# One kernel of attention and experts: the order of VectorE's and ScalarE's work within a unit, and of the experts' turns

## The chip, the cores and the metric

The kernel runs on one core of one Trainium2 chip. The metric is the device time of one execution in microseconds (us). The kernel before took 897.06 us, the median of three runs (889.57, 897.35 and 897.06).

## The reference

A layer norm feeds two branches, whose outputs are added to the input. Shapes are 4 sequences of 1024 tokens of 128 channels; 16 heads of 8 channels; 8 experts with hidden size 256, two chosen for each token.

```
xn = layernorm(x)
# attention
s = q @ k.T ; s = s - mean(s) ; s = s / mean(|s|) * gain          # over all 1024 keys
r = max(where(causal, s, -1000), 0) ** 4
y = (r / sum(r)) @ v ; attention = y @ W_proj + b_proj
# experts, two of eight by token
z = (xn @ w1 + b1) * (xn @ w2 + b2)
s = silu(z @ wg + bg) ; expert = s @ w3 + b3
out = x + attention + sum of weight * expert
```

## The kernel before

**Units.** The main loop runs over `ALL` = 192 units: 16 quads of four heads, 12 units each. A unit n is one pair of a block of 128 keys and a half of 512 queries, for four heads. `STEPS` lists them; the blocks on the diagonal are narrower, so that positions 0 to 11 in a quad have 512, 384, 256, 128, then five times 512, then 384, 256, 128 columns. For each head of a unit TensorE makes scores (line L921), ScalarE writes `U` = relu(score) (L788), VectorE writes `W` = relu(score) times `U` (L1177), GpSimd masks the diagonal and squares one part of `W` (L660, L669), ScalarE squares the rest (L799), and two units later TensorE multiplies `W` and `U` with `VS` and a column of ones into the accumulator (`average`, L859).

**Pieces.** The mean of |s| wants the sum of the positive scores over all keys. What the units don't cover is made as "pieces" of 512 scores (L914), which are only summed, by VectorE ("V", L1169, into `junk_V`) or by ScalarE ("A", L780, into `junk_A`). `PLAN` says how many pieces lie in a unit and who takes each; up to unit 35 all are VectorE's.

**Expert turns.** 39 tiles of 256 tokens (20 pairs, the last of one tile) pass through the experts in 119 turns, spread evenly over units 35 to 179, at most one in a unit. Turns of a pair p are `tx` (transpose of the tokens, L890), `m` for each tile (two products, m1 and m2, L874), `ga` and `gb` (the gate products, L894) and `my` (the last product, L899). ScalarE evacuates tx, m1, ga and gb. VectorE evacuates m2 into `zT` (L1127) and my into `yb` (L1135). GpSimd weights `yb` (L628) and scatters its rows (L635) in the units that follow. `NWB` buffers hold the experts' weights, loaded by SyncE.

**Order.** Each engine's queue is written out by the same loop. TensorE, in unit n: pieces, four scores, the turn's product, `average` of unit n-2. ScalarE: its pieces, `U`, evacuation of the turn of unit n, squares of unit n-1. VectorE: its pieces, `W`, evacuation of the turn of unit n.

**Banks.** All products but the accumulator share a ring of `NBANK` = 7 PSUM banks, in the order of `takers`: pieces, scores and turn of a unit, then of the next. An m turn takes two banks, every other turn one. Before TensorE writes a bank it waits for the reader of what stood there seven takers ago:

```
def wait_bank(engine, *who):
    if PLACE[who] >= NBANK:
        engine.wait_ge(*last_read(takers[PLACE[who] - NBANK]))
```

With three pieces a unit has seven takers, so the fourth score of a unit stands seven takers behind the last bank of the turn of the unit ahead; with four pieces, the third score does.

Of the kernel before, what the change touches and what calls it, by code (L numbers as in the profile page):

```python
# [18 lines left out]
HALF = 512  # L19
# [15 lines left out]
def layer_kernel(nc, x, w_attn, b_attn, w_proj, b_proj, score_gain, gate_w, gate_b, w_expert, out):  # L35
# [48 lines left out]

    PLAN = ["VA", "VAV", "VAV", "VAVA", "V", "V", "V", "V", "VA", "VAV", "VAV", "VAVA"]
    EARLY = 3
# [14 lines left out]

    NXT, NWB, NYB = 6, 3, 4
    NPAIR = -(-NX // 2)
    tiles_of = lambda p: range(2 * p, min(2 * p + 2, NX))
    TURNS = []
    for p in range(NPAIR):
        TURNS += [("tx", p)] + [("m", i) for i in tiles_of(p)] + [("ga", p), ("gb", p), ("my", p)]
    FFN_FROM, FFN_TO = SCATTERS // PER_STEP + 3, ALL - 12
# [27 lines left out]
    with ctx:  # L136
# [80 lines left out]
        gat = sb("gat", [P, 2, NT, C])  # L217
        pad = NWB * WW + 2 * (2 * R + 2 * R + 4 * R + 4 * R) - 2 * NT * C
        sb("rest_of_ffn", [P, pad])
# [177 lines left out]
        def _(sp):  # L397
# [68 lines left out]
            chosen = []  # L466
            W_AT = [STEP_OF["m", i] - 8 if i < NWB else STEP_OF["my", (i - NWB) // 2] + 1 for i in range(NX)]
            T_AT = [max(SCATTERS // PER_STEP + 1, STEP_OF["tx", i // 2] - 4) for i in range(NX)]
# [76 lines left out]
        def _(pool):  # L545
# [99 lines left out]
            for n in range(ALL):  # L645
                if 0 < n * PER_STEP < SCATTERS:
                    pool.wait_ge(w_done, 4 * n - 2)
                for k in range(n * PER_STEP, min(SCATTERS, (n + 1) * PER_STEP)):
                    scatter(k // NT, k % NT)
                for back in range(1, 5):  # L650
                    for kind, p in FFN_AT[n - back] if n >= back else []:
                        if kind == "my":
                            if back == 1:
                                rows_of_pair(p)
                            if back <= 2 * len(tiles_of(p)):
                                give_back(p, back - 1)
                slot, w = W[n % NU], HALF - LOW[n % NS]
# [24 lines left out]
        def _(act):  # L682
# [79 lines left out]
            for n in range(ALL + AVLAG + 2):  # L762
                y = n - AVLAG - 1
                if y >= 0 and y % NS in ENDS:
# [7 lines left out]
                    act.copy(yq[q % 2][:, STEPS[y % NS][0], :], acc).then_inc(acc_ev, 1)  # L772
                if n < ALL:
                    for m, e in PIECE_AT[n]:
                        if e == "A":
                            act.wait_ge(p_ready, m + 1)
                            k_th, at = PIECE_COUNT[m]["A"], 0
                            wait(act, p_used["A"], k_th - 1)
                            for g, _, _, w, col in PIECES[m % NP]:
                                last = act.activation(junk["A"][k_th % 2][:, at:at + w], piece(m)[:, at:at + w], ACT.Relu,  # L780
                                                      accum_out=msum[:, m // NP, g, col:col + 1])
                                at += w
                            last.then_inc(p_used["A"], 1)
                    w = HALF - LOW[n % NS]
                    wait(act, used, n - NU + 1)
                    for g in range(4):
                        act.wait_ge(s_ready, 4 * n + g + 1)
                        act.activation(U[n % NU][:, g, 0:w], score(4 * n + g)[:, 0:w], ACT.Relu).then_inc(u_ready, 1)  # L788
                    for kind, i in FFN_AT[n]:
# [179 lines left out]
        def _(vec):  # L969
# [192 lines left out]
            for n in range(ALL):  # L1162
                for m, e in PIECE_AT[n]:
                    if e == "V":
# [3 lines left out]
                        for g, _, _, w, col in PIECES[m % NP]:  # L1168
                            last = vec.tensor_scalar(junk["V"][k_th % 2][:, at:at + w], piece(m)[:, at:at + w], 0.0, None,  # L1169
                                                     ALU.max, ALU.add, accum_out=msum[:, m // NP, g, col:col + 1])  # L1170
                            at += w
                        last.then_inc(p_used["V"], 1)
                w = HALF - LOW[n % NS]
                wait(vec, used, n - NU + 1)
                for g in range(4):
                    vec.wait_ge(u_ready, 4 * n + g + 1)
                    vec.scalar_tensor_tensor(W[n % NU][:, g, 0:w], score(4 * n + g)[:, 0:w], 0.0,  # L1177
                                             U[n % NU][:, g, 0:w], ALU.max, ALU.mult).then_inc(w_done, 1)
                for kind, i in FFN_AT[n]:
                    evacuate(kind, i)  # L1180
                for b in side(n, S_SCALE):
# [64 lines left out]
```

## Time and profile before

| what | value |
|---|---|
| median of three runs | 897.06 us (889.57 to 897.35) |
| profiled execution | 888.43 us, its span 886.7 us |
| mean granted clock of TensorE in it | 0.942 of full speed |
| TensorE busy | 740.6 us, 84% of the span |
| VectorE busy | 724.4 us, 82% |
| ScalarE busy | 683.5 us, 77% |
| GpSimd busy | 623.9 us, 70% |
| largest group, VectorE's W (L1177) | 373.8 us in 768 instructions |

The profiled execution belongs to one run; its own time is 8.6 us below the median of the three. Engine names in rows: PE is TensorE, PEld its weight loads, DVE VectorE, ACT ScalarE, POOL GpSimd, SP SyncE. A row's idle time is what its engine waited just before it, and the name behind the arrow is what ended the wait.

### The profile page before, as it was taken

The numbers are of one execution on the slowest core, as the hardware profiler recorded it, in microseconds if no ns is written. First come the engines' busy times: TensorE is split into PE (matmuls) and PEld (weight loads), VectorE is DVE, ScalarE is ACT, GpSimd is POOL, SyncE is SP. The second block draws the span as 40 slices with busy tenths as digits, with TensorE's granted clock in tenths as the row PEclk, the third lists the DMA queues.
The fourth block names the chain that finished last, engine by engine and source line by source line (L and its number), as shares of the span: only waits on it lengthen the run. The fifth ranks groups of instructions, "written<-read, shape, count | busy, mean of one in ns | idle before, by whom it ended". The sixth has DMA issues, their size and how long they took to land.

```text
span 886.7 us, 17644 instructions
## 1 busy us (share of the span) xinstructions
PE 740.6 (84%) x5719; PEld 335.2 (38%) x5719; DVE 724.4 (82%) x2043; ACT 683.5 (77%) x1639; POOL 623.9 (70%) x545
## 2 busy tenths in 40 slices
PE   0572888888999999899898989989999999989872
PEld 0530222222444454444344344444434444443222
DVE  7689898989777978786876977787787977778896
ACT  0573888888987878898886787888888887878870
POOL 5262777884897687686876776787777777778773
PEclk9995797979998999999999899999999999999895
DMA  8449703155325304250523423252323605230703
GB/s 270 136 190 264 307 32 85 43 156 156 59 83 167 114 18 131 84 129 19 141 85 59 146 72 70 90 141 85 58 91 99 179 11 141 82 57 10 215 6 101
DMA packets 60330, 97.10 MB, mean 110 GB/s; under 512 B 7360, under 2 KB 39744, under 8 KB 60240
## 3 DMA queue, kind: packets, MB, share of 16 engines
q1 hardware_dynamic: 54544, 86.22, 34.1%
q0 software_dynamic: 4544, 9.38, 3.3%
q8 instruction: 45, 0.74, 0.4%
q10 hardware_dynamic: 1152, 0.40, 0.2%
q14 instruction: 45, 0.37, 0.1%
HBM read 61.29 MB, written 34.36 MB: 108 GB/s over the span
## 4 chain that ended last, share of the span: by engine, by line
PE 45%; DVE 23%; ACT 13%; issue 12%; POOL 4%; DMA 1%; DVEq 1%; SPq 0%; ACTq 0%; POOLq 0%
PE bank L859 19%; DVE W L1177 10%; PE bank L894 7%; ACT U L788 7%; PE bank L874 6%; DVE junk_V L1169 5%; PE bank L914 4%; PE bank L899 3%; ACT W L799 3%; PE bank L921 2%; ACT junk_A L780 2%; POOL W L660 1%; POOL W L669 1%; DVE zT L1127 1%; POOL sorted_x L610 1%
## 5 line engine op out<-in xcount | busy, mean ns | idle before, releaser
L1177 DVE SCALAR_TENSOR_TENSOR W<-bank,U 128x512 f32<-128x512 f32 (+3 forms) x768 | 373.8, 549 | 40.1 <-ACT U L788 38.0
L788 ACT ACTIVATE U<-bank 128x512 f32<-128x512 f32 (+3 forms) x768 | 318.5, 519 | 48.3 <-PE bank L921 35.3
L859 PE MATMUL bank<-W,VS 128*10 128x512 f32 (+3 forms) x1536 | 297.8, 507 | 13.5 <-ACT yq L772 7.2
L859 PE MATMUL bank<-U,usel 128*10 128x512 f32 (+3 forms) x1536 | 292.7, 507 | 0.0
L1169 DVE TENSOR_SCALAR_CACHE_REDUCE junk_V<-bank 128x512 bf16<-128x512 f32 (+3 forms) x445 | 218.3, 533 | 88.2 <-PE bank L914 87.5
L669 POOL TENSOR_TENSOR W<-W 128x1024 f32<-128x1024 f32 (+2 forms) x159 | 231.6, 1460 | 53.9 <-DVE W L1177 45.9
L660 POOL TENSOR_TENSOR W<-W,causal 128x512 f32<-128x512 f32 x128 | 163.6, 1278 | 108.5 <-DVE W L1177 106.9
L799 ACT ACTIVATE W<-W 128x256 f32<-128x256 f32 (+2 forms) x225 | 191.6, 880 | 10.4 <-POOL W L660 10.2
L921 PE MATMUL bank<-QS,KS 48*128 48x512 bf16 (+3 forms) x768 | 162.9, 337 | 39.3 <-DVE W L1177 17.3
L780 ACT ACTIVATE junk_A<-bank 128x512 bf16<-128x512 f32 (+3 forms) x195 | 87.7, 460 | 57.2 <-PE bank L914 56.8
L914 PE MATMUL bank<-KS,QS 48*128 48x512 bf16 (+3 forms) x640 | 102.0, 328 | 17.0 <-DVE junk_V L1169 8.5
L921 PEld LDWEIGHTS bank<-QS,KS 48*128 48x128 bf16 x768 | 56.4, 95 | 110.8 <-DVE W L1177 60.8
L859 PEld LDWEIGHTS bank<-U,usel 128*10 128x10 f32 x1536 | 59.5, 92 | 86.2 <-issue 79.4
L635 POOL DMA_INDIRECT weighted_y<-yb,row_to x78 | 79.3, 1016 | 14.7 <-issue 9.0
L874 PE MATMUL bank<-xT,wb 128*128 128x256 f32 x312 | 82.1, 409 | 7.0 <-DVE junk_V L1169 4.6
L914 PEld LDWEIGHTS bank<-KS,QS 48*128 48x128 bf16 x640 | 29.2, 95 | 153.8 <-issue 109.5
L894 PE MATMUL bank<-zT,wb 128*128 128x256 f32 x312 | 78.8, 396 | 7.6 <-DVE junk_V L1169 5.5
L859 PEld LDWEIGHTS bank<-W,VS 128*10 128x10 f32 x1536 | 59.9, 92 | 66.3 <-issue 36.9
L610 POOL DMA_INDIRECT sorted_x<-xn_row,pos x64 | 62.8, 981 | 18.0 <-issue 14.5
L874 PEld LDWEIGHTS bank<-xT,wb 128*128 128x128 f32 x312 | 58.9, 199 | 24.6 <-issue 16.9
L894 PEld LDWEIGHTS bank<-zT,wb 128*128 128x128 f32 x312 | 57.0, 193 | 24.9 <-issue 13.9
L758 ACT ACTIVATE sT<-bank,wb 128x256 f32<-128x256 f32 x78 | 33.3, 483 | 20.4 <-PE bank L894 20.3
(158 smaller groups left out, 604.5 us busy)
## 6 DMA issues: line engine op xcount, KB each, us to landing
wb<-in_experts SPq DMA_DIRECT2D x39, 707.0 KB
qk_stacked<-parts SPq DMA_DIRECT2D x8, 768.0 KB, 11.7
QS<-qk_stacked SPq DMA_DIRECT2D x32, 192.0 KB
KS<-qk_stacked SPq DMA_DIRECT2D x32, 192.0 KB
xt_all<-sorted_x SPq DMA_DIRECT2D x39, 130.0 KB, 6.0
qk_stacked<-parts SPq DMA_DIRECT2D x8, 512.0 KB, 11.7
gat<-weighted_y SPq DMA_DIRECT2D x8, 512.0 KB, 6.6
sorted_x<-xt_all SPq DMA_DIRECT2D x3, 1300.0 KB, 11.7
```

Of the source, the lines that this page charges most:

```text
L660: pool.tensor_tensor(slot[:, :, 0:P], slot[:, :, 0:P], causal[:, :].unsqueeze(1).to_broadcast([P, 4, P]), ALU.mult).then_inc(w_mask, 1)
L669: pool.tensor_tensor(some, some, some, ALU.mult).then_inc(r_ready[n % NU], 1)
L780: last = act.activation(junk["A"][k_th % 2][:, at:at + w], piece(m)[:, at:at + w], ACT.Relu, accum_out=msum[:, m // NP, g, col:col + 1])
L788: act.activation(U[n % NU][:, g, 0:w], score(4 * n + g)[:, 0:w], ACT.Relu).then_inc(u_ready, 1)
L799: act.activation(some, some, ACT.Square).then_inc(r_ready[y % NU], 1)
L859: last = pe.matmul(acc[32 * g:32 * g + VW, lo:HALF], usel[:, :] if of_u else VS[q % 2][:, j, g, :], (U if of_u else W)[n % NU][:, g, 0:HAL ...
L874: last = pe.matmul(bank_of(part, k)[:, h * R:(h + 1) * R], w[:, at + h * P:at + (h + 1) * P], moving, start=True, stop=True)
L894: last = pe.matmul(to[:, at:at + R], w[:, in_w:in_w + P], zT[k % 2][:, i % 2, h, :], start=(h == 0), stop=(h == 1))
L914: last = pe.matmul(piece(m)[:, at:at + w], QS[par][in_rows[g % 2], g // 2, P * t:P * (t + 1)], KS[par][in_rows[g % 2], g // 2, k:k + w], s ...
L921: pe.matmul(score(4 * n + g)[:, 0:HALF - lo], KS[par][in_rows[g % 2], g // 2, P * j:P * (j + 1)], QS[par][in_rows[g % 2], g // 2, HALF * c ...
L1169: last = vec.tensor_scalar(junk["V"][k_th % 2][:, at:at + w], piece(m)[:, at:at + w], 0.0, None, ALU.max, ALU.add, accum_out=msum[:, m // ...
L1177: vec.scalar_tensor_tensor(W[n % NU][:, g, 0:w], score(4 * n + g)[:, 0:w], 0.0, U[n % NU][:, g, 0:w], ALU.max, ALU.mult).then_inc(w_done, 1)
```

## The change

VectorE's queue in unit n becomes: its pieces, evacuation of the turn of unit n-1, `W`. ScalarE's becomes: `U`, its pieces, evacuation of the turn of unit n, squares. The pieces' table puts V ahead of A within a unit, with the same number of each. The turns of two pairs are interleaved, so that `my` of pair p-1 lies between the two m turns of pair p, and `tx` of pair p+1 between the second m and `ga`. GpSimd's weighting and scatters of a pair begin one unit later, a fourth weight buffer is added, and a weight load is issued one unit later after the `my` that frees its buffer.

```diff
-    PLAN = ["VA", "VAV", "VAV", "VAVA", "V", "V", "V", "V", "VA", "VAV", "VAV", "VAVA"]
+    PLAN = ["VA", "VVA", "VVA", "VVAA", "V", "V", "V", "V", "VA", "VVA", "VVA", "VVAA"]
...
-    NXT, NWB, NYB = 6, 3, 4
+    NXT, NWB, NYB = 6, 4, 4
...
-    TURNS = []
+    TURNS = [("tx", 0)]
     for p in range(NPAIR):
-        TURNS += [("tx", p)] + [("m", i) for i in tiles_of(p)] + [("ga", p), ("gb", p), ("my", p)]
+        first, *second = [("m", i) for i in tiles_of(p)]
+        TURNS += [first] + [("my", p - 1)] * (p > 0) + second + [("tx", p + 1)] * (p + 1 < NPAIR) + [("ga", p), ("gb", p)]
+    TURNS.append(("my", NPAIR - 1))
...
-            W_AT = [STEP_OF["m", i] - 8 if i < NWB else STEP_OF["my", (i - NWB) // 2] + 1 for i in range(NX)]
+            W_AT = [STEP_OF["m", i] - 8 if i < NWB else STEP_OF["my", (i - NWB) // 2] + 2 for i in range(NX)]
...
-                for back in range(1, 5):
+                for back in range(2, 6):
...
                 if n < ALL:
+                    w = HALF - LOW[n % NS]
+                    wait(act, used, n - NU + 1)
+                    for g in range(4):
+                        act.wait_ge(s_ready, 4 * n + g + 1)
+                        act.activation(U[n % NU][:, g, 0:w], score(4 * n + g)[:, 0:w], ACT.Relu).then_inc(u_ready, 1)
                     for m, e in PIECE_AT[n]:
...
-                    w = HALF - LOW[n % NS]
-                    wait(act, used, n - NU + 1)
-                    for g in range(4):
-                        act.wait_ge(s_ready, 4 * n + g + 1)
-                        act.activation(U[n % NU][:, g, 0:w], score(4 * n + g)[:, 0:w], ACT.Relu).then_inc(u_ready, 1)
...
                         last.then_inc(p_used["V"], 1)
+                for kind, i in FFN_AT[n - 1] if n else []:
+                    evacuate(kind, i)
                 w = HALF - LOW[n % NS]
...
-                for kind, i in FFN_AT[n]:
-                    evacuate(kind, i)
```

VectorE's queue around units 36 to 38, before. The first two rows evacuate m2 of unit 36; then come the two pieces and `W` of unit 37, m2 of unit 37, and the first piece of unit 38.

```order
L1127 SCALAR_TENSOR_TENSOR zT0<-bank2,wb0,x1_0 128x256 [waits ffn_m1_evacuated,ffn_m2_done]
L1127 SCALAR_TENSOR_TENSOR zT0<-bank2,wb0,x1_0 128x256
L1169 TENSOR_SCALAR junk_V1,msum<-bank3 128x512 [waits piece_used_vec,piece_ready]
L1169 TENSOR_SCALAR junk_V0,msum<-bank0 128x512 [waits piece_used_vec,piece_ready]
L1177 SCALAR_TENSOR_TENSOR W1<-bank1,U1 128x384 [waits u_ready,u_and_r_used]
L1177 SCALAR_TENSOR_TENSOR W1<-bank1,U1 128x384 [waits u_ready]
L1177 SCALAR_TENSOR_TENSOR W1<-bank2,U1 128x384 [waits u_ready] x2
L1127 SCALAR_TENSOR_TENSOR zT0<-bank0,wb1,x1_1 128x256 [waits ffn_m1_evacuated,ffn_m2_done]
L1127 SCALAR_TENSOR_TENSOR zT0<-bank0,wb1,x1_1 128x256
L1169 TENSOR_SCALAR junk_V1,msum<-bank0 128x512 [waits piece_used_vec,piece_ready]
```

The same place after the change. The pieces of a unit now stand ahead of the evacuation of the unit before it, and that one ahead of `W`.

```order
L1171 TENSOR_SCALAR junk_V1,msum<-bank3 128x512 [waits piece_used_vec,piece_ready]
L1171 TENSOR_SCALAR junk_V0,msum<-bank0 128x512 [waits piece_used_vec,piece_ready]
L1129 SCALAR_TENSOR_TENSOR zT0<-bank2,wb0,x1_0 128x256 [waits ffn_m1_evacuated,ffn_m2_done]
L1129 SCALAR_TENSOR_TENSOR zT0<-bank2,wb0,x1_0 128x256
L1181 SCALAR_TENSOR_TENSOR W1<-bank1,U1 128x384 [waits u_ready,u_and_r_used]
L1181 SCALAR_TENSOR_TENSOR W1<-bank1,U1 128x384 [waits u_ready]
L1181 SCALAR_TENSOR_TENSOR W1<-bank2,U1 128x384 [waits u_ready] x2
L1171 TENSOR_SCALAR junk_V1,msum<-bank0 128x512 [waits piece_used_vec,piece_ready]
L1171 TENSOR_SCALAR junk_V0,msum<-bank1 128x512 [waits piece_used_vec,piece_ready]
L1129 SCALAR_TENSOR_TENSOR zT0<-bank0,wb1,x1_1 128x256 [waits ffn_m1_evacuated,ffn_m2_done]
```

TensorE's queue of unit 38 up to its turn, before: three pieces, four scores, and the start of ga.

```order
L914 MATMUL bank0<-KS1,QS1 128x512 [waits piece_used_vec]
L914 MATMUL bank1<-KS1,QS1 128x512 [waits w_done] x2
L921 MATMUL bank2<-QS1,KS1 128x256 [waits w_done] x2
L921 MATMUL bank3<-QS1,KS1 128x256 [waits ffn_m1_evacuated]
L921 MATMUL bank0<-QS1,KS1 128x256 [waits ffn_m2_evacuated]
L894 MATMUL bank0<-zT0,wb0 128x256 [waits piece_used_vec,ffn_m2_evacuated]
```

The same place in the changed kernel.

```order
L916 MATMUL bank0<-KS1,QS1 128x512 [waits piece_used_act]
L916 MATMUL bank1<-KS1,QS1 128x512 [waits w_done] x2
L923 MATMUL bank2<-QS1,KS1 128x256 [waits w_done] x2
L923 MATMUL bank3<-QS1,KS1 128x256 [waits ffn_m1_evacuated]
L923 MATMUL bank0<-QS1,KS1 128x256 [waits ffn_m2_evacuated]
L892 MATMUL bank0<-ident,xt_all 128x128 [waits ffn_x_in2,piece_used_vec]
```

Pieces and scores stay where they were, and so does the wait of the fourth score (the last row but one) for the evacuation of m2 of unit 37; the turn behind it is tx where it was ga.

ScalarE's queue of unit 37 before: piece, `U`, and the squares behind them.

```order
L780 ACTIVATE junk_A0,msum<-bank0 128x512 [waits piece_used_act,piece_ready]
L788 ACTIVATE U1<-bank1 128x384 [waits scores_ready,u_and_r_used]
L788 ACTIVATE U1<-bank1 128x384 [waits scores_ready]
L788 ACTIVATE U1<-bank2 128x384 [waits scores_ready] x2
L799 ACTIVATE W0<-W0 128x1024 [waits w_masked] x2
```

ScalarE's queue from the evacuation of m1 of unit 36 through unit 37 in the changed kernel.

```order
L752 ACTIVATE x1_0<-bank2,wb2 128x256 [waits ffn_m2_evacuated,ffn_m1_done]
L752 ACTIVATE x1_0<-bank2,wb2 128x256
L780 ACTIVATE U1<-bank1 128x384 [waits scores_ready,u_and_r_used]
L780 ACTIVATE U1<-bank2 128x384 [waits scores_ready] x2
L780 ACTIVATE U1<-bank3 128x384 [waits scores_ready]
L787 ACTIVATE junk_A0,msum<-bank1 128x512 [waits piece_used_act,piece_ready]
L801 ACTIVATE W0<-W0 128x1024 [waits w_masked] x2
```

The piece has moved from ahead of `U` to behind it.

## Rows read from the trace of the kernel before

**Rows 1.** The page, part 1: busy time, share, instructions of each engine.
```profile
PE 740.6 (84%) x5719; PEld 335.2 (38%) x5719; DVE 724.4 (82%) x2043; ACT 683.5 (77%) x1639; POOL 623.9 (70%) x545
```

**Rows 2.** The page, part 4: the chain that ended last.
```profile
PE 45%; DVE 23%; ACT 13%; issue 12%; POOL 4%; DMA 1%; DVEq 1%; SPq 0%; ACTq 0%; POOLq 0%
```

**Rows 3.** Windows: the stretch with expert turns; busy us of each engine, then clock.
```profile
core 0: us, PE busy (x) PEld busy (x) DVE busy (x) ACT busy (x) POOL busy (x), PEclk, DMA share, GB/s
...
280.00:760.00 480.00, 442.28 (x3530) 214.45 (x3522) 383.23 (x1048) 393.77 (x1010) 355.78 (x310) 0.98 0.34 94
```

**Rows 4.** Waits, 280 to 790 us: total us, times, longest.
```profile
DVE junk_V L1169 <- PE bank L914: 65.3, 59, 2.4
...
DVE W L1177 <- ACT U L788: 29.4, 62, 1.3
```

**Rows 5.** Timeline, unit 37: start, us, engine, instruction, idle time before it.
```profile
219.69 0.60 PE L914 MATMUL bank<-KS,QS 48*128 48x512 bf16 x3
...
220.16 0.86 DVE L1127 SCALAR_TENSOR_TENSOR zT<-bank,wb,x 128x256 f32<-128x256 f32 x2
...
220.95 0.68 DVE L1169 TENSOR_SCALAR_CACHE_REDUCE junk_V<-bank 128x512 bf16<-128x512 f32 x1
...
221.08 0.33 PE L921 MATMUL bank<-QS,KS 48*128 48x384 bf16 x1 [0.45 <-DVE zT L1127]
...
221.78 1.97 PE L874 MATMUL bank<-xT,wb 128*128 128x256 f32 x8 [0.36 <-DVE junk_V L1169]
```

**Rows 6.** Timeline, units 81 and 82.
```profile
402.74 0.86 DVE L1127 SCALAR_TENSOR_TENSOR zT<-bank,wb,x 128x256 f32<-128x256 f32 x2
...
403.23 0.60 PE L914 MATMUL bank<-KS,QS 48*128 48x512 bf16 x3
...
403.46 0.70 PE L921 MATMUL bank<-QS,KS 48*128 48x384 bf16 x4
403.65 0.69 DVE L1169 TENSOR_SCALAR_CACHE_REDUCE junk_V<-bank 128x512 bf16<-128x512 f32 x1
...
404.50 1.97 PE L874 MATMUL bank<-xT,wb 128*128 128x256 f32 x8 [0.34 <-DVE junk_V L1169]
...
404.88 1.95 DVE L1177 SCALAR_TENSOR_TENSOR W<-bank,U 128x384 f32<-128x384 f32 x4
...
408.23 0.55 PE L914 MATMUL bank<-KS,QS 48*128 48x512 bf16 x4
...
409.50 1.97 PE L894 MATMUL bank<-zT,wb 128*128 128x256 f32 x8 [0.45 <-DVE junk_V L1169]
...
409.96 1.41 DVE L1177 SCALAR_TENSOR_TENSOR W<-bank,U 128x256 f32<-128x256 f32 x4
```

**Rows 7.** Timeline, unit 83, of four pieces.
```profile
413.24 0.61 PE L914 MATMUL bank<-KS,QS 48*128 48x256 bf16 x8
...
413.66 0.42 DVE L1169 TENSOR_SCALAR_CACHE_REDUCE junk_V<-bank 128x256 bf16<-128x256 f32 x1 [2.29 <-PE bank L914]
...
414.50 0.23 PE L921 MATMUL bank<-QS,KS 48*128 48x128 bf16 x1 [0.54 <-DVE junk_V L1169]
...
414.69 1.97 PE L894 MATMUL bank<-zT,wb 128*128 128x256 f32 x8
```

**Rows 8.** Timeline, unit 60, a unit of one piece on each engine.
```profile
319.13 0.39 PE L914 MATMUL bank<-KS,QS 48*128 48x512 bf16 x2
...
319.89 1.99 PE L894 MATMUL bank<-zT,wb 128*128 128x256 f32 x8
...
320.88 2.48 DVE L1177 SCALAR_TENSOR_TENSOR W<-bank,U 128x512 f32<-128x512 f32 x4 [0.62 <-ACT U L788]
```

**Rows 9.** The line of yb: instructions, ns min/median/max, first and last start.
```profile
L1135 DVE TENSOR_TENSOR yb<-bank,wb x39: 410/411/426, 241.0 to 815.6; 128x256 f32<-128x256 f32 x39
```

**Rows 10.** Windows before and in a fall of the clock, columns as in rows 3.
```profile
148.00:151.00 3.00, 1.32 (x7) 0.43 (x11) 3.00 (x7) 3.00 (x5) 2.01 (x4) 1.00 0.07 22
151.00:154.50 3.50, 3.50 (x20) 0.59 (x13) 2.60 (x6) 3.50 (x7) 2.59 (x4) 0.57 0.17 51
```

More of the change, by code:

```diff
@@ L217, in layer_kernel @@
         gat = sb("gat", [P, 2, NT, C])
-        pad = NWB * WW + 2 * (2 * R + 2 * R + 4 * R + 4 * R) - 2 * NT * C
+        pad = NWB * (WW + 10) + 2 * (2 * R + 2 * R + 4 * R + 4 * R) - 2 * NT * C
         sb("rest_of_ffn", [P, pad])
@@ L649, in _ @@
                     scatter(k // NT, k % NT)
-                for back in range(1, 5):
+                for back in range(2, 6):
                     for kind, p in FFN_AT[n - back] if n >= back else []:
                         if kind == "my":
-                            if back == 1:
+                            if back == 2:
                                 rows_of_pair(p)
-                            if back <= 2 * len(tiles_of(p)):
-                                give_back(p, back - 1)
+                            if back - 2 < 2 * len(tiles_of(p)):
+                                give_back(p, back - 2)
                 slot, w = W[n % NU], HALF - LOW[n % NS]
```

## The prediction

> **What bounds the kernel now.** I read the page first: TensorE is busy 84% of the span, VectorE 82%, ScalarE 77% [rows 1], and the chain that ended last lies on TensorE for 45% and on VectorE for 23% [rows 2]. An average hides stages, so next the windows. Up to unit 35 nothing that the change touches happens (all pieces are VectorE's, there is no turn, and `U` has no piece to pass), and units behind 180 have no turn. In the stretch with turns TensorE is busy 442.3 of 480 us at a granted clock of 0.98 [rows 3]. So it idles 37.7 us there; that is nearly all that a better order could win, and every new wait of TensorE is added to the time, unless another engine is late at the same place.
>
> VectorE is what TensorE's order leans on. It waits 65.3 us for pieces, 59 times, and 29.4 us for `U`, 62 times [rows 4]. The first of these waits matters: behind `W`, VectorE has nothing to do until TensorE has finished turn and average, and in that gap it now evacuates the turn. Unit 80's m2 is evacuated from 402.74 to 403.60 while TensorE averages and begins the pieces of unit 81 at 403.23 [rows 6]. That evacuation costs nothing.
>
> **VectorE: the evacuation behind the next unit's pieces.** Seven banks make a ring. In a unit of three or four pieces the fourth or third score uses the bank of the turn of the unit ahead. The order of the changed kernel shows it for unit 38: its last score waits for m2 of unit 37, and VectorE now comes to that only behind its two pieces of unit 38. The same wait stands in the kernel before, where it is mostly long over. Where it isn't, the trace has its signature: in unit 37 VectorE ends m2 of unit 36 at 221.02 and the score starts at 221.08, 0.45 us late [rows 5]. So a freed bank is used 0.06 us later.
>
> The price, by unit 82 [rows 6]. TensorE starts its pieces at 408.23, VectorE has summed its pieces at 409.96 (there `W` starts). Now m2 of unit 81 follows, 0.86 us as at 402.74: 410.82. The score starts 0.06 us later, and the turn 0.19 us behind it (414.50 to 414.69, [rows 7]): 411.07, where it started at 409.50. That is 1.57 us; taken as 1.55. For `my` the evacuation is two instructions of 0.41 us [rows 9]: in unit 81 VectorE's pieces end at 404.88, so 404.88 + 0.82 + 0.06 + 0.19 = 405.95 against 404.50 [rows 6], 1.45 us. A unit of four pieces has the same columns for VectorE, and its turn starts 1.45 us behind its first piece [rows 7], not earlier than the 1.27 us in unit 82; I take the same price. VectorE can't catch up behind it: `W` of unit 82 would end 0.9 us later, but TensorE's next pieces come 1.5 us later.
>
> How often: from the two tables of turns and takers, a score of the next unit stands on the bank of an m2 in 19 units and on that of a `my` in 10. The count was 29 before too; what changes is VectorE's place in each. Five of these lie in position 1 of a quad, where VectorE is late already. In unit 37 the turn started 2.09 us behind the first piece [rows 5]. With the new order VectorE goes to the pieces at 220.16, needs 1.23 us for them (403.65 to 404.88, [rows 6]), then 0.86 + 0.06 + 0.19: 222.50 against 221.78, 0.7 us. The sum: 15 x 1.55 + 9 x 1.45 + 5 x 0.7 = 39.8, say **+39**. A stall that falls into one that exists would cost nothing, and the full price is the other end: 0 to 45.
>
> **Smaller terms of the same kind.** In positions 0 and 8 (two pieces) it is the next turn that stands on the bank. In unit 60 the turn starts at 319.89, 0.76 us behind the first piece at 319.13 [rows 8]; VectorE would free the bank about 0.43 + 0.62 + 0.86 + 0.06 = 1.97 us behind it. That is 1.2 us in seven units, and 7 with some of it hidden behind VectorE in position 0. In units of four pieces the turn waits for VectorE's second piece where it waited for ScalarE's first, some 0.4 us in the 12 of them that have no stall yet: 5. ScalarE's pieces are now read behind `U`, so that their banks come free some 2 us later; only with a short turn or none is TensorE there by then: 2. Together **+14** (3 to 20).
>
> **ScalarE: U ahead of its pieces.** In unit 60 `W` waits 0.62 us for `U`, which stands behind a piece [rows 8]. That wait goes, but in most units VectorE then waits for TensorE anyway. I count 0.4 us in 13 units of position 0, **-5**, with 0 and the whole 29.4 us [rows 4] as ends. The pieces' table (V ahead of A) leaves counts alone and lets VectorE begin both its pieces sooner; without it the stall would be longer, and it has no price of its own.
>
> **Interleaved turns, GpSimd, SyncE.** The number of turns, their products and their spacing stay. `ga` gets tx between it and the m2 that it needs; this covers the later evacuation, and without it `ga` would wait as the scores do. `my` lies at least one turn further from `gb`. GpSimd's weighting and its scatters come one unit later; behind them in its queue are the mask and the square of the same unit, as before, and their cover is two units until the average. The fourth buffer lets each weight load be issued some four units ahead of its m turn; its wait stands in SyncE's queue ahead of loads of tokens and of a quad's stores and loads. TensorE waited for no weight load in this trace. I cost these at nothing; if the cover were gone, one late load in each of 20 pairs would cost about a microsecond each (0 to 20).
>
> **The clock.** At 148 to 151 us TensorE was busy 1.32 of 3.00 us, and in the 3.5 us that follow the granted clock was 0.57, mostly its lower level of 1.2 GHz [rows 10]. A fall costs (1 - 0.57) x 3.5 = 1.5 us of its work. The stretch with turns has few falls now (0.98, [rows 3]), and its idle time comes in bits of half a microsecond. The new stalls are 1.6 us idle in one piece at 24 places. I take five falls, **+8**; 0 to 30 are the ends.
>
> The Trainium skill (TensorE: Matmul & The Clock Gate, A second HAM failure mode: psum-queue depth-cycling) says that a kernel which cycles through PSUM banks can leave TensorE idle so often for short times that its clock goes up and down. By that rule the falls would be many and not five, which is the second rival below; the rows of the stretch with turns don't show it so far.
>
> **The sum.** 39 + 14 - 5 + 8 = +56. On the profiled execution (888.4) this gives 944. The three runs lie at 889.6, 897.1 and 897.4; their median is 8.6 us above the profiled one. Since either level may come, I add to the middle of the runs, 893.5: **950 us**. Its own range is 930 to 970.
>
> **The rivals.**
> 1. *Half absorbed.* TensorE's existing idle 37.7 us are partly at the same scores, and VectorE, which enters each unit free, may do its pieces sooner than in these rows. With half of 39 and 14, no falls and -5: 893.5 + 21 = 915. For it: unit 37, where half the price was there already. Against: only five of 29 places lie in that position.
> 2. *The clock falls at most stalls.* 15 more falls of 1.5 us: 950 + 22 = 972. For it: rows 10. Against: one fall needs not follow each stall; the windows at 148 had idle time of more than one wait.
> 3. *Faster.* ScalarE's `U` first is the edit that counts: VectorE waits 29.4 us for it, and if VectorE is the engine that ends the units, about half of that goes straight to the end, with evacuations hidden while `U` is made: 893.5 - 16 = 877. The point from which it decides: the last score of a unit would have to come 2.5 us behind its first piece anyway, so that the evacuation is over. In unit 82 the turn, behind all scores, starts at 1.27 us [rows 6], so the rows speak against it.
> 4. *No change.* Stalls and savings cancel, the order of TensorE being bound by the sum of its products: 893.
>
> **Chances.** Forecast 0.52, half absorbed 0.20, clock 0.12, faster 0.08, no change 0.08. Slower by over 1% (which is about what a measurement of this kernel can tell from no change) holds the first three: 0.84. The range reaches from 905 (below the first rival) to 985 (above the second, for the ends of the clock's term) and leaves out the last two.
>
> **What would show it.** In the profile after: TensorE's scores waiting for zT and yb, 29 times and about 1.6 us each, some 40 us where there were few; VectorE's wait for pieces longer; its wait for `U` shorter; TensorE's share of the stretch with turns near 0.86 and more slices of its clock below 9. Wrong would be: waits for zT of half a microsecond, or a fourth score that starts no later than before; then VectorE reaches the evacuation sooner than I think, or another engine sets the pace.

## The result and the profile after

The changed kernel takes 980.43 us, the median of four runs (975.05 to 980.80), against 894.60 us for four runs of the kernel before (889.57 to 897.35). The ratio is 1.0952, with an interval of 1.0884 to 1.1021. The profiled execution took 980.13 us, with a span of 978.4 us and a mean clock of 0.91 (before: 888.43, 886.7 and 0.942).

First the page: engines (part 1) and the chain that ended last (part 4), which answer to [rows 1, 2].

```profile
PE 776.8 (79%) x5719; PEld 347.7 (36%) x5719; DVE 721.6 (74%) x2043; ACT 689.3 (70%) x1639; POOL 623.8 (64%) x545
...
PE 54%; DVE 25%; issue 12%; ACT 7%; DMA 1%; DVEq 1%; SPq 0%; ACTq 0%
```

TensorE's busy time rose from 740.6 to 776.8 us with the same 5719 matmuls, so 36.2 us are the same work at a lower clock. The rest of the span, in which TensorE is idle, rose from 146.1 to 201.6 us, by 55.5. The two make the 91.7 us of the span. VectorE and ScalarE do the same work in nearly the same time; their shares fell. The window of the stretch with turns (columns as in [rows 3], where it showed 442.28 busy and a clock of 0.98; being slower, the kernel gets through fewer units in it):

```profile
280.00:760.00 480.00, 409.64 (x3061) 195.64 (x3060) 331.14 (x916) 347.70 (x891) 307.68 (x267) 0.93 0.29 81
```

The same work is compared by taking each kernel from its first score of unit 35 to its first score of unit 180, here before and then after:

```profile
212.11:819.71 607.60, 557.27 (x4453) 268.86 (x4451) 483.55 (x1342) 499.95 (x1286) 454.98 (x391) 0.98 0.32 89
```

```profile
216.04:911.60 695.56, 593.73 (x4453) 280.72 (x4451) 481.64 (x1343) 505.04 (x1286) 453.61 (x388) 0.93 0.27 77
```

So the whole 36 us of busy time lie in this part. In the record of the granted clock it has 4 stretches at the lower level before and 25 after.

What TensorE waited for is in the view of waits (engine, line, releaser: total us, times, longest).

```profile
DVE junk_V L1171 <- PE bank L916: 204.7, 118, 4.6
...
PE bank L923 <- DVE zT L1129: 35.5, 19, 2.1
...
PE bank L923 <- DVE yb L1137: 17.4, 10, 1.9
...
DVE W L1181 <- ACT U L780: 14.0, 41, 1.3
...
PE bank L923 <- DVE junk_V L1171: 12.5, 27, 0.5
...
PE bank L896 <- DVE junk_V L1171: 8.0, 18, 0.6
...
PE bank L916 <- ACT junk_A L787: 5.3, 7, 1.3
```

The evacuations of zT and yb now hold up scores in 19 and 10 places, for 35.5 and 17.4 us: 1.87 and 1.74 us each. Before, the same two releasers stood ahead of scores for 1.3 and 0.6 us. VectorE's wait for pieces, 87.5 us before over the whole span, is 204.7: it is free early and stands idle until TensorE gets on. Its wait for `U` fell from 38.0 to 14.0 us and bought nothing.

Unit 37 in the timeline (start us, us, engine, instruction, idle time before it) answers to [rows 5].

```profile
225.22 0.60 PE L916 MATMUL bank<-KS,QS 48*128 48x512 bf16 x3
...
225.64 0.69 DVE L1171 TENSOR_SCALAR_CACHE_REDUCE junk_V<-bank 128x512 bf16<-128x512 f32 x1 [0.41 <-PE bank L916]
...
226.87 0.87 DVE L1129 SCALAR_TENSOR_TENSOR zT<-bank,wb,x 128x256 f32<-128x256 f32 x2
227.66 1.94 DVE L1181 SCALAR_TENSOR_TENSOR W<-bank,U 128x384 f32<-128x384 f32 x4
...
227.80 0.33 PE L923 MATMUL bank<-QS,KS 48*128 48x384 bf16 x1 [1.65 <-DVE zT L1129]
...
228.06 2.83 PE L876 MATMUL bank<-xT,wb 128*128 128x256 f32 x8
```

TensorE begins its pieces at 225.22, VectorE has summed both at 226.87, evacuates m2 of unit 36 until 227.74, and 0.06 us later the fourth score starts, 1.65 us late. The turn starts 2.84 us behind the first piece; before it was 2.09. The turn itself then takes 2.83 us where it took 1.97. That is the clock, and unit 38 shows it again behind the next stall: these are its fourth score and a row of two matmuls of the average that follows, 0.60 us at the upper level.

```profile
234.60 0.28 PE L923 MATMUL bank<-QS,KS 48*128 48x256 bf16 x1 [1.77 <-DVE zT L1129]
...
236.64 1.07 PE L861 MATMUL bank<-W,VS 128*10 128x512 f32 x2
```

The windows of these units (columns as in [rows 3]) put the clock beside it.

```profile
225.00:229.00 4.00, 2.35 (x19) 1.31 (x12) 3.59 (x10) 2.82 (x8) 3.16 (x2) 1.00 0.00 0
229.00:232.00 3.00, 3.00 (x23) 1.55 (x24) 0.59 (x2) 2.08 (x6) 2.25 (x2) 0.51 0.00 0
232.00:235.00 3.00, 1.23 (x9) 0.44 (x6) 2.56 (x8) 1.54 (x5) 0.50 (x1) 0.92 0.11 20
235.00:238.50 3.50, 3.50 (x21) 0.65 (x21) 0.86 (x3) 2.10 (x5) 2.48 (x3) 0.63 0.80 169
```

TensorE is busy 2.35 of 4.00 us around the first stall, and then 3 us are granted at 0.51, the lower level of 1.2 GHz; it is busy 1.23 of 3.00 us around the second, and 0.63 follows. Of the 29 stalls, 1.53 to 2.07 us long, 19 have a stretch at the lower level that begins within 2 us of the score that ends them; the other ten have none. [rows 10] showed the same pattern in the kernel before, in a part without turns.

### The profile page after: what moved, and what is told of

It is laid out like the page before. It is cut to its first block, busy times and chain, and to the rows that moved or that the text cites. A ratio compares the mean times of both kernels' runs of the same rounds, so it can differ in the third digit from the quotient of the medians.

```text
span 978.4 us, 17644 instructions
## 1 busy us (share of the span) xinstructions
PE 776.8 (79%) x5719; PEld 347.7 (36%) x5719; DVE 721.6 (74%) x2043; ACT 689.3 (70%) x1639; POOL 623.8 (64%) x545
## 4 chain that ended last, share of the span: by engine, by line
PE 54%; DVE 25%; issue 12%; ACT 7%; DMA 1%; DVEq 1%; SPq 0%; ACTq 0%
PE bank L861 22%; PE bank L876 8%; DVE W L1181 8%; PE bank L896 8%; DVE junk_V L1171 7%; PE bank L916 5%; PE bank L901 4%; PE bank L923 3%; ACT U L780 3%; DVE zT L1129 3%; ACT W L801 2%; DVE yb L1137 1%; ACT junk_A L787 1%; PE bank L832 1%; DMA x_t<-in_L_attn_x 1%
## 5 line engine op out<-in xcount | busy, mean ns | idle before, releaser
L780 ACT ACTIVATE U<-bank 128x512 f32<-128x512 f32 (+3 forms) x768 | 323.5, 510 | 192.6 <-PE bank L923 176.3
L1171 DVE TENSOR_SCALAR_CACHE_REDUCE junk_V<-bank 128x512 bf16<-128x512 f32 (+3 forms) x445 | 218.7, 534 | 204.9 <-PE bank L916 204.7
L861 PE MATMUL bank<-W,VS 128*10 128x512 f32 (+3 forms) x1536 | 313.8, 529 | 14.2 <-ACT W L801 7.1
L861 PE MATMUL bank<-U,usel 128*10 128x512 f32 (+3 forms) x1536 | 308.7, 530 | 0.0
L923 PE MATMUL bank<-QS,KS 48*128 48x512 bf16 (+3 forms) x768 | 163.0, 337 | 78.9 <-DVE zT L1129 35.5
L916 PE MATMUL bank<-KS,QS 48*128 48x512 bf16 (+3 forms) x640 | 106.0, 334 | 24.0 <-DVE junk_V L1171 9.1
L876 PE MATMUL bank<-xT,wb 128*128 128x256 f32 x312 | 88.0, 427 | 8.3 <-DVE junk_V L1171 4.4
L896 PE MATMUL bank<-zT,wb 128*128 128x256 f32 x312 | 81.1, 404 | 11.0 <-DVE junk_V L1171 8.0
L901 PE MATMUL bank<-wb,sT 128*128 128x128 f32 x312 | 47.0, 313 | 3.7 <-DVE zT L1129 2.5
## 6 DMA issues: line engine op xcount, KB each, us to landing
sorted_x<-xt_all SPq DMA_DIRECT2D x3, 1300.0 KB, 11.5
```

The source lines that it names most:

```text
L861: last = pe.matmul(acc[32 * g:32 * g + VW, lo:HALF], usel[:, :] if of_u else VS[q % 2][:, j, g, :], (U if of_u else W)[n % NU][:, g, 0:HAL ...
L876: last = pe.matmul(bank_of(part, k)[:, h * R:(h + 1) * R], w[:, at + h * P:at + (h + 1) * P], moving, start=True, stop=True)
L896: last = pe.matmul(to[:, at:at + R], w[:, in_w:in_w + P], zT[k % 2][:, i % 2, h, :], start=(h == 0), stop=(h == 1))
L916: last = pe.matmul(piece(m)[:, at:at + w], QS[par][in_rows[g % 2], g // 2, P * t:P * (t + 1)], KS[par][in_rows[g % 2], g // 2, k:k + w], s ...
L923: pe.matmul(score(4 * n + g)[:, 0:HALF - lo], KS[par][in_rows[g % 2], g // 2, P * j:P * (j + 1)], QS[par][in_rows[g % 2], g // 2, HALF * c ...
```

## The experiments

Theory: VectorE's evacuation behind the next unit's pieces makes the loss, through the bank that a score of that unit wants, partly as idle time and partly through the clock that falls behind it. Rival A: ScalarE's `U` first costs too, since its pieces' banks come free late. Rival B: the interleaved turns cost. Rivals C and D: the clock's falls follow the idle time and count, or they don't. The kernels ran on three chips, each beside the kernel before: the changed kernel with the evacuation in its own unit and the three "before" kernels down to the pieces' table beside one of 892.91 us, the turns alone, the evacuation behind the first piece, the average first and the three zero matmuls beside one of 907.45, the rest beside one of 905.74. So ratios are compared and not times, and the forecasts, made in us beside about 895, are read as ratios too.

| kernel | ratio to before | interval |
|---|---|---|
| changed | 1.0952 | 1.0884 to 1.1021 |
| changed, evacuation in its own unit | 1.0141 | 1.0101 to 1.0180 |
| before, evacuation moved alone | 1.0867 | 1.0820 to 1.0913 |
| before, U first alone | 1.0503 | 1.0438 to 1.0569 |
| before, U first and the pieces' table | 1.0091 | 1.0055 to 1.0127 |
| before, turns, buffer, GpSimd's rows alone | 0.9982 | 0.9943 to 1.0020 |
| changed, evacuation behind the first piece | 1.0536 | 1.0503 to 1.0568 |
| changed, average ahead of the blocked score | 1.0402 | 1.0367 to 1.0437 |
| changed, three zero matmuls in the stall | 1.0879 | 1.0846 to 1.0912 |
| changed, two | 1.0668 | 1.0619 to 1.0717 |
| changed, one | 1.0633 | 1.0585 to 1.0681 |
| changed, again, beside those two | 1.0845 | 1.0792 to 1.0898 |
| changed, evacuation by unit | 1.0207 | 1.0159 to 1.0254 |

**The evacuation back in its own unit.**

```diff
-                for kind, i in FFN_AT[n - 1] if n else []:
-                    evacuate(kind, i)
                 w = HALF - LOW[n % NS]
...
+                for kind, i in FFN_AT[n]:
+                    evacuate(kind, i)
                 for b in side(n, S_SCALE):
```

> The changed kernel with VectorE's evacuation of the turn put back behind W of its own unit; U first, the pieces' table, the turns, the fourth buffer stay. Theory (the evacuation behind the next unit's pieces makes the whole loss, by the ring of banks): TensorE's 29 waits for zT and yb go from 52.9 us to under 4, its busy time from 777 back to about 740 since the clock falls less, and the time is 885 to 902. Rival A (U ahead of ScalarE's pieces frees their banks late and costs too): 905 to 925. Rival B (the interleaved turns cost): the same 905 to 925, told apart by the kernels with one part each.

Measured: 904.98 us, ratio 1.0141. Scores wait for zT 2.6 us in all, 6 times, and for yb not at all; TensorE's busy time is back (page, part 1):

```profile
PE 735.9 (82%) x5719; PEld 333.3 (37%) x5719; DVE 724.6 (81%) x2043; ACT 685.4 (76%) x1639; POOL 623.4 (69%) x545
```

So this one placement carries eight of the nine and a half per cent, with all of the clock's part. 1.4% stay: 904.98 lies above the 885 to 902 of the theory and at the edge of rival A's 905 to 925, and as a ratio (1.012 to 1.034) inside it. Rival A holds for this rest, as the kernel with `U` first and the table shows below.

**The evacuation moved alone,** with the opposite diff on the kernel before.

> The kernel before with one edit: VectorE evacuates the turn of unit n-1 between pieces and W of unit n. The old turns also have 29 scores on a bank of m2 or my. Theory: 29 waits of 1.6 to 1.9 us each and as many falls of the clock, and ga behind the second m now waits for zT in units where it follows at once: 965 to 990. Rival (the loss needs the interleaved turns or U first with it): below 940.

Measured: 969.93 us, ratio 1.0867. The waits (columns as above):

```profile
PE bank L921 <- DVE zT L1127: 35.5, 19, 2.1
...
PE bank L921 <- DVE yb L1135: 17.2, 10, 2.0
...
PE bank L894 <- DVE zT L1127: 10.5, 9, 1.2
```

The time lies in the 965 to 990 that I expected. These are the same 19 and 10 places and the same sizes as in the changed kernel, with the old turns. So it needs neither the interleaved turns nor `U` first. The third row is what the interleaving is for: without tx between the second m and ga, nine ga turns wait 10.5 us for zT.

**U first alone.**

```diff
                 if n < ALL:
+                    w = HALF - LOW[n % NS]
+                    wait(act, used, n - NU + 1)
+                    for g in range(4):
+                        act.wait_ge(s_ready, 4 * n + g + 1)
+                        act.activation(U[n % NU][:, g, 0:w], score(4 * n + g)[:, 0:w], ACT.Relu).then_inc(u_ready, 1)
                     for m, e in PIECE_AT[n]:
                         if e == "A":
...
```

> The kernel before with one edit: ScalarE makes U ahead of its pieces. My prediction put -5 us on it (889); VectorE's wait for U falls from 38 us to about 14. Rival A: ScalarE's pieces are summed up to 2 us later, TensorE waits for their banks, and the time is 900 to 915.

Measured: 936.07 us, ratio 1.0503. I had expected a gain of 5 us; this is the largest miss of the study. It is beyond rival A too, which gave 900 to 915. Who waited for ScalarE's pieces (L785 in this kernel), from the view of that line:

```profile
  PE bank L874: 16.0, 18
...
  PE bank L894: 9.6, 8
  PE bank L914: 9.1, 12
  PE bank L899: 3.6, 3
```

TensorE waits 38.3 us for them in these four rows; before it was 1.0. In "VAV" and "VAVA" the second piece is ScalarE's, and its bank is wanted next by the second product of an m turn or by a ga, gb, my or tx in the same unit. While the piece stood ahead of `U`, it was read in time. Behind four activations of `U` it isn't.

**U first with the pieces' table.**

```diff
-    PLAN = ["VA", "VAV", "VAV", "VAVA", "V", "V", "V", "V", "VA", "VAV", "VAV", "VAVA"]
+    PLAN = ["VA", "VVA", "VVA", "VVAA", "V", "V", "V", "V", "VA", "VVA", "VVA", "VVAA"]
...
```

> The kernel before with U ahead of ScalarE's pieces and the pieces' table V ahead of A. Theory: within 1% of before (886 to 903). Rival A: as with U alone or worse, since in a unit of four pieces the turn waits for VectorE's second piece: 900 to 915.

Measured: 900.60 us, ratio 1.0091, within the 1% that I expected. The table gives back four of the five per cent: VectorE's second piece now stands on the bank that is wanted first. What is left of the waits:

```profile
PE bank L894 <- DVE junk_V L1169: 9.9, 22, 0.6
...
PE bank L874 <- DVE junk_V L1169: 8.8, 20, 0.6
...
PE bank L914 <- ACT junk_A L785: 7.8, 10, 1.3
```

ga, gb (L894) and m (L874) wait 18.7 us for VectorE's pieces, where these two waited 10.1 before, and pieces (L914) wait 7.8 us for ScalarE's. Together, `U` first and its table cost 0.9% and save no time. TensorE's idle time, span less busy time, is 161.8 us here and 161.7 in the changed kernel with the evacuation in its own unit, where it was 146.1 before: the rest that stayed there is mainly this pair.

**The turns alone.** The kernel before with `NXT, NWB, NYB`, `TURNS`, `W_AT` and `range(2, 6)` of the change.

> The kernel before with the interleaved turns, the fourth weight buffer, the later weight loads and GpSimd's rows one unit later; VectorE's and ScalarE's queues and the pieces' table as before. Theory: ga no longer waits for zT (1.3 us before), nothing else: 885 to 900. Rival B: the turns bring waits of their own: 905 or more.

Measured: 905.00 us beside 907.45, ratio 0.9982: no difference. The time alone would touch rival B's 905, but the kernel before is slower on this chip. Rival B falls. The parts add up: 8.7% for the evacuation, 0.9% for `U` and table, nothing for the turns, against 9.5% for all.

**Behind the first piece.** The evacuation stands ahead of VectorE's second piece.

```diff
...
                         last.then_inc(p_used["V"], 1)
-                for kind, i in FFN_AT[n - 1] if n else []:
-                    evacuate(kind, i)
+                        if not evacuated:
+                            evacuated = True
+                            for kind, i in FFN_AT[n - 1] if n else []:
+                                evacuate(kind, i)
```

> The changed kernel with the evacuation moved ahead of VectorE's second piece, behind its first. In units of three or four pieces the bank comes free 0.6 to 0.7 us sooner. Theory (the time is the wait for the bank): the 29 waits fall from 1.8 to 1.2 us each, 18 us less, and the clock falls somewhat less often: 945 to 965. Rival C (the clock falls at any such stall and its falls are most of the loss): 965 to 978. If the stall isn't on the path: 980.

Measured: 952.67 us, ratio 1.0536. The theory gave 945 to 965 beside about 895, ratios of 1.056 to 1.079, so this is a little better than forecast. Its waits, and then the page's row of TensorE:

```profile
PE bank L923 <- DVE zT L1129: 23.3, 19, 1.4
...
PE bank L923 <- DVE yb L1137: 10.9, 10, 1.3
```

```profile
PE 757.8 (80%) x5719; PEld 336.5 (35%) x5719; DVE 721.8 (76%) x2043; ACT 689.8 (73%) x1639; POOL 623.1 (66%) x545
```

The 29 waits fell by 18.7 us to 34.2, as expected. TensorE's busy time is 757.8 us, where two profiles of the changed kernel have 776.8 and 773.2, and the turns alone, on the same chip as this one, 746.4. A stall shorter by a third lost half of the clock's part or more: the two shrink together, not one for the other. The stretches at the lower level between units 35 and 180 are 9, where those two profiles have 25 and 18.

**Zero matmuls in the stall.** They read `U` against a stationary of zeros and add nothing to the accumulator, so the result is the same.

```diff
                     for g in range(4):
+                        of = takers[PLACE["score", 4 * n + g] - NBANK] if PLACE["score", 4 * n + g] >= NBANK else ("", 0)
+                        if of[0] in ("m2", "my") and of in [(k if k != "m" else "m2", i) for k, i in FFN_AT[n - 1]] and n % NS in (1, 3, 9, 10, 11):
+                            for _ in range(3):
+                                pe.matmul(acc[0:9, 0:HALF], usel[:, 0:9], U[(n - 3) % NU][:, 0, :], start=False, stop=False,
+                                          skip_group_check=True)
                         wait_bank(pe, "score", 4 * n + g)
```

> The changed kernel with three matmuls of 512 columns against a stationary of zeros, added to the accumulator (they add nothing), ahead of the score that waits for the bank, in 23 of the 29 places (position 2 of a quad is left out). They take about 1.3 us and lie in the stall. Rival C (falls of the clock follow the idle time and cost TensorE 36 us of busy time): the clock stays at its upper level, the time falls by 20 to 35 us, to 945 to 960, although work is added. Rival D (the clock falls for another reason, or its falls are hidden in other waits): 978 to 990.

Measured: 984.39 us, ratio 1.0879. The time lies in rival D's 978 to 990, the ratio between the two forecasts, and it can't be told from the changed kernel's. The timeline shows why: three of them (six instructions) run 2.74 us and not the 1.3 that I had reckoned with, and the score that waited for a bank before starts right behind them without a wait.

```profile
410.40 2.74 PE L925 MATMUL bank<-U,usel 128*9 128x512 f32 x6
413.08 0.33 PE L928 MATMUL bank<-QS,KS 48*128 48x384 bf16 x1
413.34 1.99 PE L876 MATMUL bank<-xT,wb 128*128 128x256 f32 x8
```

They add some 0.9 us to each of 23 stalls, about 20 us. The page's row of TensorE has the gain that this hides:

```profile
PE 818.8 (83%) x5857; PEld 348.1 (35%) x5857; DVE 723.2 (74%) x2043; ACT 688.9 (70%) x1639; POOL 623.0 (63%) x545
```

Without 23 x 2.74 us the kernel's own matmuls take 755.8, some 20 us less than in the changed kernel. Then two and one of them were run, with the changed kernel beside them.

> The changed kernel with two of the zero matmuls, not three, ahead of the blocked score in 23 of the 29 places. Three took 2.74 us in the trace, 0.9 us more than the wait that they fill; two take 1.83 us, about the wait. Rival C (the clock's falls follow the idle time): added work is hidden and the falls are mostly gone, 20 to 30 us below the changed kernel run beside it. Rival D (the clock doesn't matter): no more than 3 us from it.

> The same with one zero matmul, 0.91 us of a wait of 1.8 us. It can add nothing to the path. Rival C: the idle time in one piece is halved, and 10 to 30 us of the clock's falls go; rival D: no change from the changed kernel.

> The changed kernel itself, on the chip of the two kernels with zero matmuls, to compare them on one chip: its ratio to the kernel before again 1.09 to 1.10.

Measured: two 966.36 us (1.0668), one 964.57 us (1.0633), the changed kernel 982.75 us (1.0845). Work was added, and 16 us went with two (20 to 30 were expected, at most 3 by rival D), 18 us with one (10 to 30 expected). TensorE's row on the page of the changed kernel on this chip, then with one, then with two:

```profile
PE 773.2 (79%) x5719; PEld 343.7 (35%) x5719; DVE 722.6 (74%) x2043; ACT 689.9 (70%) x1639; POOL 623.9 (64%) x545
```

```profile
PE 774.9 (81%) x5765; PEld 335.0 (35%) x5765; DVE 722.5 (75%) x2043; ACT 688.3 (72%) x1639; POOL 623.0 (65%) x545
```

```profile
PE 792.7 (82%) x5811; PEld 340.8 (35%) x5811; DVE 722.7 (75%) x2043; ACT 688.9 (71%) x1639; POOL 623.9 (65%) x545
```

One zero matmul (two instructions) is 1.03 us of busy time in the timeline below, so 23 of them are 23.7 us of the 774.9; the kernel's own matmuls took 751.2, against 773.2 without: 22 us less. The idle time fell from 206.8 to 185.2 us, which is about the zero matmuls' own time. So the score starts as late as it did, and what went is the slower clock behind it. Between units 35 and 180 (windows as above, the changed kernel on this chip, then with one):

```profile
227.45:913.08 685.63, 581.76 (x4451) 275.42 (x4448) 481.78 (x1343) 504.89 (x1286) 453.62 (x388) 0.95 0.27 78
```

```profile
225.03:891.03 666.00, 582.41 (x4497) 267.92 (x4493) 481.66 (x1343) 503.71 (x1286) 453.13 (x388) 0.98 0.28 80
```

Less 23.7, the own matmuls take 558.7 us there, against 557.27 in the kernel before: all of the clock's part is gone. The stretches at the lower level fell from 18 to 5. In unit 37 of the kernel with one, the turn that had taken 2.83 us takes 1.99:

```profile
233.47 1.03 PE L925 MATMUL bank<-U,usel 128*9 128x512 f32 x2
235.19 0.33 PE L928 MATMUL bank<-QS,KS 48*128 48x384 bf16 x1 [0.70 <-DVE zT L1134]
235.46 1.99 PE L876 MATMUL bank<-xT,wb 128*128 128x256 f32 x8
```

That decides for rival C: the clock's falls follow TensorE's idle time in the stalls, and they cost on the path. Whether it is the length of one piece of idle time that counts or its sum around the place is not shown; a zero matmul shortens both. Two of them take 1.89 us:

```profile
237.31 1.89 PE L925 MATMUL bank<-U,usel 128*9 128x512 f32 x4
239.13 0.33 PE L928 MATMUL bank<-QS,KS 48*128 48x384 bf16 x1
```

Then the kernel's own matmuls take 792.7 - 23 x 1.89 = 749.2 us, about the same as with one.

**The average ahead of the blocked score.** TensorE does the average of unit n-2 in the stall and not behind the turn.

```diff
                     for g in range(4):
+                        of = takers[PLACE["score", 4 * n + g] - NBANK] if PLACE["score", 4 * n + g] >= NBANK else ("", 0)
+                        if not averaged and of in [(k if k != "m" else "m2", i) for k, i in (FFN_AT[n - 1] if n else []) if k in ("m", "my")]:
+                            averaged = True
+                            averages(n - AVLAG)
                         wait_bank(pe, "score", 4 * n + g)
...
```

> The changed kernel in which TensorE, in the 29 units whose third or fourth score stands on the bank of the turn ahead, does the average of unit n-2 ahead of that score and not behind the turn. The average (0.6 to 1.8 us) fills the stall. Theory: most of the wait and of the clock's falls go: 905 to 935, the rest being later U and W of those units. If the bank isn't the reason: 980.

Measured: 942.61 us beside 907.45, ratio 1.0402. I had expected 905 to 935 beside about 895, ratios up to 1.045. What is left of the scores' waits for zT and yb, 35.5 and 17.4 us before:

```profile
PE bank L937 <- DVE zT L1137: 8.4, 10, 1.1
...
PE bank L937 <- DVE yb L1145: 3.0, 6, 1.0
```

```profile
PE 765.0 (81%) x5719; PEld 340.9 (36%) x5719; DVE 721.1 (77%) x2043; ACT 686.7 (73%) x1639; POOL 623.2 (66%) x545
```

Real work in the stall takes away more than half of the loss, which confirms the bank. Beside the turns alone (902.28 us in its profiled execution, on the same chip; this one 943.28), TensorE is busy 18.6 us more and idle 22.4 us more. The two rows above are 9.3 us of that (11.4 against 2.1), and pieces now wait 11.1 us for ScalarE's pieces, where they waited for none; the rest was not taken apart.

**By unit.** The evacuation lies behind the next unit's pieces only for turns of positions 3 to 7, otherwise in its own unit.

```diff
-                for kind, i in FFN_AT[n - 1] if n else []:
+                for kind, i in FFN_AT[n - 1] if n and n % NS in range(4, 9) else []:
                     evacuate(kind, i)
...
+                for kind, i in FFN_AT[n] if (n + 1) % NS not in range(4, 9) else []:
+                    evacuate(kind, i)
                 for b in side(n, S_SCALE):
```

> The changed kernel, but VectorE's evacuation lies behind the pieces of the next unit only where the next unit has few pieces and no score on the turn's bank (turns of positions 3 to 7, followed by positions 4 to 8); elsewhere it is behind W of its own unit. Theory (only the 29 places cost): as the kernel with all evacuations in their own unit, ratio 1.00 to 1.02 to the kernel before. If the place of the evacuation costs in every unit: 1.03 or more.

Measured: 924.56 us, ratio 1.0207, just above the expected 1.00 to 1.02, with an interval (1.0159 to 1.0254) that begins inside it. That is 0.7 points above all evacuations in their own unit (1.0141, on another chip), and the two intervals overlap. So nearly all of the loss sits in the units of positions 0 to 3 and 9 to 11, where the 29 places lie.

## Why the prediction was right, and where its sizes were off

The direction and the mechanism held. I wrote that "a score of the next unit stands on the bank of an m2 in 19 units and on that of a `my` in 10", and the trace has 19 and 10 waits, each ended by the evacuation, with the score 0.06 us behind it. The size was off: the forecast of 950 us had its own range of 930 to 970, and 980.43 lies outside it, inside the wider 905 to 985, whose upper end was set by the clock's term. The second rival of the prediction, many falls of the clock (972), came nearest in time.

The mis-sized term is **the clock**. I took five falls, +8 us, with 30 as the far end. It measured 36.2 us more busy time for the same matmuls, with 21 stretches at the lower level more than before between units 35 and 180. In a second profile of the changed kernel, on another chip, there are 18 stretches instead of 25, and there one zero matmul in 23 stalls takes 22 us away again. The row was in front of me: behind 1.32 busy of 3.00 us the clock had gone to 0.57 [rows 10], and the stalls that I had just worked out leave TensorE as idle as that. Having shown the pattern, I had no row for expecting it in only five of 24 places. What the Trainium skill tells of a kernel that cycles through PSUM banks (TensorE: Matmul & The Clock Gate, A second HAM failure mode: psum-queue depth-cycling), that frequent short idle times of TensorE make its clock go up and down, pointed the right way. The trace agrees, with 0.93 of full clock between 280 and 760 us where it was 0.98.

**The evacuation.** In unit 37 I had the turn 2.81 us behind the first piece (222.50 against 219.69); it came after 2.84. Scores waited 51.0 us longer for zT and yb, and 11.5 us less for `junk_V` and `W` (17.1 and 17.3 us before, 12.5 and 10.4 after): net 39.5, where I had +39. The sum of +39 and +14 less 5 makes 48 us of idle time; 55.5 came, and most of the difference is the -5, which didn't come.

**U ahead of the pieces, and the table.** Here the reasoning was wrong and the total hid it, by luck. I wrote that `U` first gives -5 us and that the table "has no price of its own". `U` first alone costs 5.0%, and the table is what pays four of the five back. I had priced the late banks of ScalarE's pieces at 2 us, by the changed kernel, where the table had already moved them; taken apart, the edit and its cover are each large. The pair costs 0.9%, some 8 us, where my terms for it (-5, and 5 and 2 of the smaller ones) made +2.

**Turns, GpSimd, SyncE** cost nothing, as forecast: 0.9982. The cover that I named for `ga` is real: without it, nine ga turns wait 10.5 us.

**The rivals.** Half absorbed (915): no, the existing idle time was elsewhere. Faster (877): VectorE's wait for `U` did fall, from 38.0 to 14.0 us, and turned into wait for pieces.

Three things stay open: whether the rest of 1.4% with the evacuation in its own unit holds more than the 0.9% of `U` and table (the intervals of the two meet), which property of the idle time the clock's falls follow, and part of what keeps the kernel with the average first at 4%. No version here beats the kernel before.

## What to carry to other kernels

When banks go round in a ring, an evacuation has a due time set by who writes its bank next, not by who reads its result; before it is moved behind other work, count on by as many takers as the ring has banks (seven here) and ask when that one is due. Work that an engine does in a gap is free only there. On the engine that sets the pace, price a new stall twice: its own length, and the slower clock that may follow it, here 36 us on top of 55.

## What the runs showed of the hardware that was not expected

Stalls of 1.53 to 2.07 us on TensorE were followed by a stretch at the lower level at 19 of 29 places (0.51 and 0.63 of full clock in the windows above), and at 14 of 29 in the second profile of the changed kernel. With the stalls shortened to 0.92 to 1.39 us it was 5 of 29. One useless matmul of 1 us in such a stall made the kernel 18 us faster; in unit 37 the idle time that was left ahead of the score was 0.70 us.
